# A transformer block in hyperbolic space on one core: one VectorE operation in place of two for q and k, and for the pair of gated MLP tiles

## The chip, the cores and the metric

The kernel runs on one core of a Trainium2 chip. The metric is the device time of one execution in microseconds (us), lower is better.

## The reference

The input x is 128 sequences of 64 tokens with 256 features, cond one row of 256 per sequence. All of it is float32. Vectors live in a ball: `logmap0` scales a vector by arctanh(norm)/norm, `expmap0` by tanh(norm)/norm, and a projection is `plin(x, w, b) = expmap0(logmap0(x) @ w + b)`. Cut to what matters:

```python
sh_msa, sc_msa, g_msa, sh_mlp, sc_mlp, g_mlp = split(t_emb @ w_ada + b_ada, 6)
xm = expmap0(layer_norm(logmap0(x)) * (1 + sc_msa) + sh_msa)
q, k, v = (_to_heads(plin(xm, w, b)) for w, b in ((w_q, b_q), (w_k, b_k), (w_v, b_v)))
qt, kt, vt = (logmap0(q), logmap0(k), logmap0(v))        # 16 heads of 16
attn = softmax(einsum('bhqd,bhkd->bhqk', qt, kt) / sqrt(16))
attn_out = plin(_from_heads(expmap0(attn @ vt)), w_o, b_o)
x1 = mobius_add(x, expmap0(g_msa * logmap0(attn_out)))
xm = expmap0(layer_norm(logmap0(x1)) * (1 + sc_mlp) + sh_mlp)
ff = plin(plin(xm, w_f1, b_f1), w_f2, b_f2)
out = x + mobius_add(x1, expmap0(g_mlp * logmap0(ff)))
```

In tangent space q, k and v of a head are the rows of the projection, each multiplied by one factor per token and head. That product for q and k is the first place of the change. The product `g_mlp * logmap0(ff)` is, up to a factor that is applied later, the second.

## The kernel before

A tile is 128 tokens (two sequences) by 256 features; there are 64. x stays in SBUF (`x_all`). The program has a setup (weights, the two MLP matrices folded into one, statistics of x), a loop over the 64 tiles for attention, a block of small operations on statistics of all tiles, and a loop over 32 pairs of tiles for the MLP and the output. Nothing is scheduled by a planner: each engine has its own stream of instructions, written by hand, and semaphores tie them together.

*Attention loop.* Slots are software-pipelined. In the slot of DVE (VectorE) in which tile n is modulated, tile n-4 gets its factors, n-6 is normalised and gated, and so on (`L_A` to `L_G`). DVE's order in a slot, each a function with one operation unless said otherwise: `limit` (L1202), `modulate` (L1081, needs rows of `mod` by DMA), `factors` (L1208), `scale_qk` (L1219, two operations), `shift_t` (L1127), `sum_squares` and `sum_rows` (L1149, L1153), `softmax_sums` (L1158), `clip_t` (L1134), `normalise` (L1163, writes `o`), `repeat_parts` (L1228, L1229), `project` (L1143, writes `u` from the qkv PSUM), `dot_x` (L1195), `gate_z` (L1188, needs the output projection in PSUM). PE (TensorE) in a slot: transpose of `t` (L839), the projection to q and k (L885), attention times v (L899), the projection to v (L885), then waits for `o` and transposes it (L850), the scores (L875) and the output projection (L856, L858), between which ScalarE copies the transposed `o` (L617). After `scale_qk`, ScalarE rounds q and k to 16 bit (L612) and GpSimd takes the rest (L478), both once for q and k together, after a wait for both. SP's queue issues, in this order in a slot, the rows of `mod` (L372), the transposing DMA of q and k (L379) and the rows of `gate` (L385). `modulate` and the sums go by tile parity in double buffers. DVE's stream is written out in full (its slots are unrolled in Python), PE's, ScalarE's, GpSimd's and SP's are hardware loops of two slots.

*MLP loop.* All engines are unrolled. DVE's order for a pair: `clip_t2` (L1354), `inner_square` for both tiles (L1362, needs PE's inner product), `inner_norm` (L1370), `first_sum` (L1273), `scale_t2` (L1282) and `shift_t2` (L1348) for both tiles of a later pair, `inner_factors` (L1376), `mlp_output` for both (L1384, writes `ff`), `gate_mlp` for both (L1393, reads `ff`), `dot_x1` for both (L1400, reads what was gated). Every fourth slot brings a chain of some twenty small operations on the factors of eight tiles (`output_norms`, `output_factors`, L1415 to L1446; called the fin chain here). ScalarE's order: scale x (L688), scale t2 by the clip (L714), diagonals (L744), copy of the transposed tile (L719), copy of the output (L749), squares of t2 (L707), of `ff` (L725) and of the gated tiles (L731). PE transposes (L933), multiplies (L947) and adds up the output (L959 to L961). 

The waits at the first place and at the second are these:

```python
dve.wait_ge(fac_ready, i + 1)          # scale_qk, before two operations
dve.wait_ge(ff_ready, n + 1)           # gate_mlp, n = 2 * i + j
dve.wait_ge(fg_ready, n + 1)           # dot_x1
```

Of the kernel before, what the change touches and what calls it, by code (L numbers as in the profile page):

```python
# [26 lines left out]
ALU = mybir.AluOpType  # L27
# [3 lines left out]
P = 128  # L31
# [21 lines left out]
def build(nc, x, cond, w_q, b_q, w_k, b_k, w_v, b_v, w_o, b_o, w_f1, b_f1, w_f2, b_f2, w_ada, b_ada, out):  # L53
    B, S, D = x.shape
    FF = w_f1.shape[1]
    H = 16
    HD = D // H
# [12 lines left out]
    with ExitStack() as ctx:  # L70
        def sb(name, shape, dt=F32):
            return ctx.enter_context(nc.sbuf_tensor(name, shape, dt))
# [4 lines left out]
        def sem(name):  # L77
            return ctx.enter_context(nc.semaphore(name))
# [12 lines left out]
        def scratch(n):  # L91
# [39 lines left out]
        u = sb("u", [P, 2, 3 * D])  # L131
# [10 lines left out]
        fac = sb("fac", [P, 3 * H])  # L142
        qk = sb("qk", [P, 2 * D])
# [19 lines left out]
        ff = qk[:, :].rearrange("p (j d) -> p j d", j=2)  # L163
        fgs = ([u[:, :, :].rearrange("p a n -> p (a n)")[:, 2 * D * n:2 * D * n + 2 * D] for n in range(3)]
               + [usq[:, 0:2 * D], tT[:, :, :, :].rearrange("p a c n -> p (a c n)"),
                  wqkv[:, :, :].rearrange("p c n -> p (c n)")[:, 4 * D:6 * D],
                  v[:, :, :, :].rearrange("p a h n -> p (a h n)")[:, 0:2 * D], wo[:, :, :].rearrange("p c n -> p (c n)")])
        fgs = [b.rearrange("p (j d) -> p j d", j=2) for b in fgs]
# [4 lines left out]
        gates2 = (gate[:, :, :], bqkv[:, 0:2 * D].rearrange("p (j d) -> p j d", j=2))  # L173
# [63 lines left out]
        qk_ready = sem("qk_ready"); high_ready = sem("high_ready"); low_ready = sem("low_ready"); again_ready = sem("again_ready"); v_ready = sem("v_ready")  # L237
# [17 lines left out]
        ff_ready = sem("ff_ready"); fg_ready = sem("fg_ready")  # L255
# [74 lines left out]
        def on2(h, off, lag):  # L330
            return not isinstance(h, int) or 0 <= TURN * h + off - lag < HALF
# [653 lines left out]
        def _(dve):  # L985
# [10 lines left out]
            n = T // 8  # L996
# [88 lines left out]
            part = lambda k: bn[:, :, k]  # L1085
# [126 lines left out]
            def scale_qk(i, k):  # L1212


                dve.wait_ge(fac_ready, i + 1)
                after(dve, low_ready, i)
                for a in range(2):
                    part = slice(a * D, a * D + D)
                    dve.tensor_tensor(qk[:, part].rearrange("p (h d) -> p h d", d=HD), u[:, k, part].rearrange("p (h d) -> p h d", d=HD),  # L1219
                                      fac[:, a * H:a * H + H].unsqueeze(2).broadcast_to([P, H, HD]), ALU.mult).then_inc(qk_ready, 1)  # L1220

            def repeat_parts(i, k, half):

# [160 lines left out]
                dve.scalar_tensor_tensor(out=ff[:, j, :], in0=(p_qkv, p_s)[k][:, 512 * j + P:512 * j + P + D], scalar=ch[:, j:j + 1],  # L1384
                                         in1=b2[:, :], op0=ALU.mult, op1=ALU.add).then_inc(ff_ready, 1)

            def gate_mlp(i, j, k, r, half):

                n = 2 * i + j
                dve.wait_ge(ff_ready, n + 1)  # L1390
                dve.wait_ge(gate2_in[k], 32 * half + 32)
                after(dve, out_psum, i - (TURN - 1))
                dve.tensor_tensor(fgs[r][:, j, :], ff[:, j, :], gates2[k][:, j, :], ALU.mult).then_inc(fg_ready, 1)  # L1393

            def dot_x1(i, j, r, q, col):

# [64 lines left out]
            def slot2(h, off):  # L1461
                slots = TURN * h + off
                if on2(h, off, M_Q):
                    clip_t2(slots - M_Q, (off - M_Q) % 2)
                if on2(h, off, M_B):
                    i, k = slots - M_B, (off - M_B) % 2
                    for j in range(2):
                        inner_square(i, j, k)
                    inner_norm(i)
                if on2(h, off, M_A):  # L1470
                    i, k = slots - M_A, (off - M_A) % 2
                    half = (TURN // 2) * h + (off - M_A) // 2
                    for j in range(2):
                        if not at_start(h, off):
                            first_sum(i, j)
                    for j in range(2):
                        if not at_start(h, off):
                            scale_t2(i, j, k, half)
                    for j in range(2):
                        shift_t2(i, j, k)  # L1480
                if group_at(h, off, M_P) is not None:
                    output_root(group_at(h, off, M_P))
                if on2(h, off, M_B):
                    i, k, r = slots - M_B, (off - M_B) % 2, (off - M_B) % TURN
                    half = (TURN // 2) * h + (off - M_B) // 2
                    q, col = parity(off, M_B), 2 * ((off - M_B) % GROUP)
                    inner_factors(i)
                    for j in range(2):
                        mlp_output(i, j, k)
                    for j in range(2):  # L1490
                        gate_mlp(i, j, k, r, half)
                    for j in range(2):
                        dot_x1(i, j, r, q, col)
                if group_at(h, off, M_N) is not None:
                    output_norms(group_at(h, off, M_N), parity(off, M_N))
                if group_at(h, off, M_P) is not None:
                    output_factors(group_at(h, off, M_P), parity(off, M_P))
# [25 lines left out]
```

## Time and profile before

| | |
|---|---|
| median of 3 runs | 765.44 us (763.75 to 766.3) |
| the profiled execution | 765.7 us |
| its span | 763.9 us |
| granted TensorE clock, mean | 0.945 |
| busy: PE, DVE, ACT, POOL | 84%, 86%, 69%, 45% of the span |
| attention loop | from about 55 to 490 us |
| MLP loop | from about 530 to 760 us |

In the profile PE is TensorE, DVE VectorE, ACT ScalarE, POOL GpSimd, SPq the DMA queue of SyncE. L1219 is line 1219 of the kernel. The shares are means over stages with different limits. "issue" is idle time in which an engine waited for nothing that the profile shows. A wait is put down to what came last. The profile's timeline joins neighbouring operations of one group in one row (x2), whose time is then that of all of them from first start to last end. The semaphore waits that stand as instructions of their own are not shown in it.

### The profile page before, as it was taken

What the parts mean: (1) busy time and instruction counts of PE and PEld (TensorE: products, weight loads), DVE (VectorE), ACT (ScalarE), POOL (GpSimd) and SP (SyncE); (2) the same over time, 40 slices, a digit from 0 to 9 for tenths busy, and PEclk for the clock granted to TensorE, in tenths of its full rate; (3) what the DMA queues carried; (4) which work ended last, traced back from release to release, by engine and by line L of the source; (5) the groups of instructions that cost most, each with busy time, mean ns of one, the idle gap of its engine ahead of it and who ended that gap; (6) DMA issues with size and microseconds to landing.
All of it is one profiled execution on the core that took longest, in us unless ns stands there. A gap on an engine that the chain in (4) does not pass through costs nothing. (4 is left out here: it accounts for less than half of the span.)

```text
span 763.9 us, 27111 instructions
## 1 busy us (share of the span) xinstructions
PE 644.4 (84%) x8419; PEld 464.3 (61%) x8433; DVE 654.1 (86%) x2171; ACT 524.7 (69%) x1563; POOL 347.0 (45%) x683
## 2 busy tenths in 40 slices
PE   4956889999999999999999997605669999999996
PEld 2645667777777777777777775402326566656664
DVE  2786788999999999999999997485998999999975
ACT  1123567777777777777777775334879989999874
POOL 1003556666666666666666665111234244234321
PEclk9978899999999999999999998656999999999999
DMA  9942876666666666666666665222444455445523
GB/s 321 359 116 57 141 131 137 146 141 143 141 147 142 145 142 147 141 141 144 147 140 147 144 133 113 50 70 70 124 124 133 139 158 163 149 132 166 164 72 110
DMA packets 184804, 107.50 MB, mean 141 GB/s; under 512 B 140188, under 2 KB 167591, under 8 KB 184744
## 3 DMA queue, kind: packets, MB, share of 16 engines
q1 hardware_dynamic: 182952, 103.99, 55.6%
q10 hardware_dynamic: 1792, 2.89, 1.0%
q8 instruction: 17, 0.28, 0.1%
q14 instruction: 43, 0.35, 0.1%
HBM read 64.11 MB, written 9.18 MB: 96 GB/s over the span
## 5 line engine op out<-in xcount | busy, mean ns | idle before, releaser
L885 PE MATMUL p_qkv<-wqkv,tT 128*128 128x256 f32 x768 | 198.1, 396 | 5.5 <-DVE u L1143 5.5
L885 PEld LDWEIGHTS p_qkv<-wqkv,tT 128*128 128x128 f32 x768 | 139.7, 195 | 22.9 <-issue 6.3
L899 PEld LDWEIGHTS p_o<-v,pT 64*64 64x64 f32 x4096 | 66.7, 136 | 21.9 <-issue 21.9
L899 PE MATMUL p_o<-v,pT 64*64 64x17 f32 x4096 | 73.0, 210 | 0.0
L858 PE MATMUL p_oz<-wo,oT 128*128 128x256 f32 x256 | 69.7, 397 | 0.0
L445 POOL TENSOR_TENSOR rt<-ss_t,c_mhalf 128x1 f32<-128x1 f32 x64 | 42.1, 658 | 60.6 <-ACT junk L634 53.7
L659 ACT ACTIVATE pT<-p_s 128x1024 f32<-128x1024 f32 x64 | 65.6, 1024 | 2.8 <-PE p_s L875 1.7
L1143 DVE SCALAR_TENSOR_TENSOR u<-p_qkv,ct,bqkv 128x768 f32<-128x768 f32 x64 | 64.3, 1005 | 3.5 <-PE p_qkv L885 3.5
L617 ACT ACTIVATE oT<-p_oz 128x256 f32<-128x256 f32 x64 | 24.6, 384 | 57.0 <-PE p_oz L850 57.0
L504 POOL TENSOR_TENSOR rt<-ss,c_mhalf 128x2 f32<-128x2 f32 x32 | 26.5, 827 | 80.8 <-ACT wqkv L707 80.8
L933 PE MATMUL p_t<-ident,pT 128*128 128x128 f32 x128 | 21.3, 290 | 46.5 <-ACT pT L714 46.5
L1149 DVE TENSOR_REDUCE hs<-usq 128x48 f32<-128x768 f32 x64 | 60.5, 945 | 0.0
L478 POOL TENSOR_TENSOR qk<-qk 128x512 f16<-128x512 f32 x32 | 37.0, 1156 | 51.4 <-ACT qk L612 51.4
L478 POOL TENSOR_TENSOR mod_b<-qk,mod_b 128x512 f16<-128x512 f32 x32 | 37.0, 1156 | 49.7 <-ACT mod_b L612 49.7
L510 POOL TENSOR_TENSOR rh<-hh,c_mhalf 128x2 f32<-128x2 f32 x32 | 27.3, 854 | 70.1 <-DVE hh L1370 70.1
L628 ACT ACTIVATE usq<-u 128x768 f32<-128x768 f32 x64 | 53.3, 833 | 6.2 <-DVE u L1143 6.2
L947 PE MATMUL p_qkv<-wff,qk 128*128 128x384 f32 (+1 forms) x128 | 53.4, 561 | 0.8 <-ACT qk L719 0.8
L947 PE MATMUL p_s<-wff,qk 128*128 128x384 f32 (+1 forms) x128 | 52.6, 555 | 0.9 <-ACT qk L719 0.9
L850 PE MATMUL p_oz<-ident,o 128*128 128x128 f32 x128 | 27.3, 296 | 29.8 <-DVE o L1163 14.8
L1219 DVE TENSOR_TENSOR qk<-u,fac 128x256 f32<-128x256 f32 x128 | 48.6, 421 | 2.2
L933 PEld LDWEIGHTS p_t<-ident,pT 128*128 128x128 f32 x128 | 13.8, 143 | 59.4 <-ACT pT L714 30.8
L858 PEld LDWEIGHTS p_oz<-wo,oT 128*128 128x128 f32 x256 | 46.4, 202 | 3.8
(275 smaller groups left out, 1685.2 us busy)
## 6 DMA issues: line engine op xcount, KB each, us to landing
mod<-mod_rows SPq DMA_DIRECT2D x128, 128.0 KB, 2.9
x_all<-in_x SPq DMA_DIRECT2D x8, 1024.0 KB, 14.3
gate<-mod_rows SPq DMA_DIRECT2D x128, 64.0 KB, 2.7
mod<-mod_rows SPq DMA_DIRECT2D x32, 256.0 KB, 4.2
mod_b<-mod_rows SPq DMA_DIRECT2D x32, 256.0 KB, 4.4
out<-x_all SPq DMA_DIRECT2D x32, 256.0 KB, 3.0
gate<-gate_rows SPq DMA_DIRECT2D x32, 128.0 KB, 2.9
bqkv<-gate_rows SPq DMA_DIRECT2D x32, 128.0 KB, 2.9
```

Source lines behind the costliest of these rows:

```text
L445: pool.tensor_tensor(rt[:, k:k + 1], ss_t[:, k:k + 1], c_mhalf[:, 0:1], ALU.pow).then_inc(rt_ready, 1)
L478: pool.tensor_tensor(low, qk[:, :].rearrange("p (a h d) -> p a h d", a=2, d=HD), big[:, :, :, 0, :], ALU.subtract).then_inc(low_ready, 1)
L628: act.activation(usq[:, :], u[:, k, :], ACT.Square).then_inc(u_squared, 1)
L659: act.activation(pT[:, :, :, :].rearrange("p e g n -> p (e g n)"), p_s[:, :], ACT.Exp, scale=SCALE / (QK_UP * QK_UP)).then_inc(p_ready, 1)
L858: mm = pe.matmul(p_oz[:, D:2 * D], oT[:, c, :, :].rearrange("p b s -> p (b s)"), wo[:, c, :], start=False, stop=c == C - 1)
L885: mm = pe.matmul(p_qkv[:, a * D:a * D + D], tT[:, k, c, :], wqkv[:, c, a * D:a * D + D], start=c == 0, stop=c == C - 1)
L899: mm = pe.matmul(p_o[S * e:S * e + S, col:col + VW], pT[keys, e, g, :], v[keys, k, 2 * g + e, :], start=True, stop=True, skip_group_check= ...
L933: mm = pe.transpose(p_t[:, m * P:m * P + P], t2s[:, k, m // 2, (m % 2) * P:(m % 2) * P + P], ident[:, :])
L947: mm = pe.matmul((p_qkv, p_s)[k][:, 512 * j + c * P:512 * j + 512], t2T[:, k, j, c, :], wff[:, c, c * P:2 * D], start=False, stop=c == C - 1)
L1143: dve.scalar_tensor_tensor(out=u[:, k, :], in0=p_qkv[:, 0:3 * D], scalar=ct[:, k:k + 1], in1=bqkv[:, :], op0=ALU.mult, op1=ALU.add).then_i ...
L1149: dve.tensor_reduce(hs[:, 0:3 * H], usq[:, :].rearrange("p (a d) -> p a d", d=HD), AX.X, ALU.add).then_inc(heads_summed, 1)
L1219: dve.tensor_tensor(qk[:, part].rearrange("p (h d) -> p h d", d=HD), u[:, k, part].rearrange("p (h d) -> p h d", d=HD), fac[:, a * H:a * H ...
```

## The change

`scale_qk` multiplies q and k (512 columns side by side in `u` and `qk`) by their factors in one operation and raises `qk_ready` by 2 at its end, instead of once after each half. `gate_mlp` gates both tiles of a pair in one operation, after a wait for both outputs, and raises `fg_ready` by 2. Nothing else is edited.

```diff
                 dve.wait_ge(fac_ready, i + 1)
                 after(dve, low_ready, i)
-                for a in range(2):
-                    part = slice(a * D, a * D + D)
-                    dve.tensor_tensor(qk[:, part].rearrange("p (h d) -> p h d", d=HD), u[:, k, part].rearrange("p (h d) -> p h d", d=HD),
-                                      fac[:, a * H:a * H + H].unsqueeze(2).broadcast_to([P, H, HD]), ALU.mult).then_inc(qk_ready, 1)
+                dve.tensor_tensor(qk[:, :].rearrange("p (h d) -> p h d", d=HD), u[:, k, 0:2 * D].rearrange("p (h d) -> p h d", d=HD),
+                                  fac[:, 0:2 * H].unsqueeze(2).broadcast_to([P, 2 * H, HD]), ALU.mult).then_inc(qk_ready, 2)
...
-            def gate_mlp(i, j, k, r, half):
-
-                n = 2 * i + j
-                dve.wait_ge(ff_ready, n + 1)
+            def gate_mlp(i, k, r, half):
+
+                dve.wait_ge(ff_ready, 2 * i + 2)
                 dve.wait_ge(gate2_in[k], 32 * half + 32)
                 after(dve, out_psum, i - (TURN - 1))
-                dve.tensor_tensor(fgs[r][:, j, :], ff[:, j, :], gates2[k][:, j, :], ALU.mult).then_inc(fg_ready, 1)
+                dve.tensor_tensor(fgs[r], ff[:, :, :], gates2[k], ALU.mult).then_inc(fg_ready, 2)
...
-                    for j in range(2):
-                        gate_mlp(i, j, k, r, half)
+                    gate_mlp(i, k, r, half)
```

On DVE in the attention loop the stream was, with the semaphores that each operation waits for in brackets (those beyond the first are instructions of their own):

```order
L1202 TENSOR_TENSOR rlim<-roots,c_lim 128x3 [waits fac_ready,roots_ready]
L1081 SCALAR_TENSOR_TENSOR lnx<-x_all,arrays,mod 128x256 [waits t_ready,mod_in1]
L1208 TENSOR_TENSOR fac<-roots,rlim 128x48 [waits v_ready,qk_ready,rlim_ready]
L1219 TENSOR_TENSOR qk<-u,fac 128x256 [waits low_ready,fac_ready]
L1219 TENSOR_TENSOR qk<-u,fac 128x256
L1127 SCALAR_TENSOR_TENSOR t<-lnx,arrays,mod 128x256 [waits t_squared,tT_psum,ln_half]
L1149 TENSOR_REDUCE hs<-usq 128x48 [waits roots_ready,u_squared]
```

and is now, in the same place:

```order
L1202 TENSOR_TENSOR rlim<-roots,c_lim 128x3 [waits fac_ready,roots_ready]
L1081 SCALAR_TENSOR_TENSOR lnx<-x_all,arrays,mod 128x256 [waits t_ready,mod_in1]
L1208 TENSOR_TENSOR fac<-roots,rlim 128x48 [waits v_ready,qk_ready,rlim_ready]
L1217 TENSOR_TENSOR qk<-u,fac 128x512 [waits low_ready,fac_ready]
L1127 SCALAR_TENSOR_TENSOR t<-lnx,arrays,mod 128x256 [waits t_squared,tT_psum,ln_half]
L1149 TENSOR_REDUCE hs<-usq 128x48 [waits roots_ready,u_squared]
```

One instruction is gone, its neighbours stand as before. In the MLP loop DVE's stream for a pair was

```order
L1376 TENSOR_SCALAR ch<-rh 128x2 [waits ff_ready,rh_ready]
L1384 SCALAR_TENSOR_TENSOR qk<-p_qkv,ch,b 128x256 [waits fg_ready,ff_squared,ch_ready] x2
L1393 TENSOR_TENSOR u<-qk,gate 128x256 [waits gate2_in0,ff_ready] x2
L1400 SCALAR_TENSOR_TENSOR junk,fst<-g_all,u 128x256 [waits xf_summed,fg_ready] x2
L1354 TENSOR_SCALAR ct<-rt 128x2 [waits t2s_ready,rt2_ready]
```

and is now

```order
L1374 TENSOR_SCALAR ch<-rh 128x2 [waits ff_ready,rh_ready]
L1382 SCALAR_TENSOR_TENSOR qk<-p_qkv,ch,b 128x256 [waits fg_ready,ff_squared,ch_ready] x2
L1390 TENSOR_TENSOR u<-qk,gate 128x512 [waits gate2_in0,ff_ready]
L1397 SCALAR_TENSOR_TENSOR junk,fst<-g_all,u 128x256 [waits xf_summed,fg_ready] x2
L1352 TENSOR_SCALAR ct<-rt 128x2 [waits t2s_ready,rt2_ready]
```

The line numbers behind each edit fall by two, then by three. The streams of the other engines are unchanged.

## Rows read from the trace of the kernel before

**Rows 1.** The page, busy us (share of the span) xinstructions
```profile
PE 644.4 (84%) x8419; PEld 464.3 (61%) x8433; DVE 654.1 (86%) x2171; ACT 524.7 (69%) x1563; POOL 347.0 (45%) x683
```

**Rows 2.** By stage: length, busy PE, PEld, DVE, ACT, POOL, PEclk, DMA share, GB/s
```profile
119.61:451.74 332.13, 311.67 (x6086) 240.55 (x6085) 313.05 (x938) 248.95 (x677) 213.04 (x469) 1.00 0.65 144
601.04:628.80 27.76, 26.45 (x104) 17.21 (x105) 25.97 (x103) 25.56 (x90) 10.34 (x10) 1.00 0.52 152
534.38:557.77 23.39, 16.05 (x53) 7.34 (x53) 22.81 (x85) 19.21 (x69) 7.58 (x9) 1.00 0.48 130
```

**Rows 3.** Timeline of DVE: start, us, line, operation, tiles, count
```profile
304.85 0.20 DVE L1208 TENSOR_TENSOR fac<-roots,rlim 128x48 f32<-128x48 f32 x1
...
311.43 0.20 DVE L1208 TENSOR_TENSOR fac<-roots,rlim 128x48 f32<-128x48 f32 x1
...
314.00 0.09 DVE L1134 TENSOR_SCALAR ct<-rt 128x1 f32<-128x1 f32 x1
314.12 0.42 DVE L1163 TENSOR_TENSOR o<-p_o,rden 128x256 f32<-128x256 f32 x1
...
316.86 0.42 DVE L1188 SCALAR_TENSOR_TENSOR g_all<-p_oz,gate 128x256 f32<-128x256 f32 x1
...
317.68 0.20 DVE L1208 TENSOR_TENSOR fac<-roots,rlim 128x48 f32<-128x48 f32 x1
317.92 0.76 DVE L1219 TENSOR_TENSOR qk<-u,fac 128x256 f32<-128x256 f32 x2
318.60 0.47 DVE L1127 SCALAR_TENSOR_TENSOR t<-lnx,arrays,mod 128x256 f32<-128x256 f32 x1
```

**Rows 4.** Timeline of PE; in brackets idle time before, and what ended it
```profile
308.54 0.41 PE L850 MATMUL p_oz<-ident,o 128*128 128x128 f32 x2 [0.61 <-DVE o L1163]
...
314.79 0.41 PE L850 MATMUL p_oz<-ident,o 128*128 128x128 f32 x2 [0.16 <-issue]
```

**Rows 5.** Waits in 119.6 to 457.7 us: in total, times, longest
```profile
DVE rden L1158 <- issue: 3.0, 13, 0.2
DVE lnx L1081 <- DMA mod<-mod_rows: 1.4, 4, 0.5
```

**Rows 6.** DMA queues in 119.61 to 451.74 us: packets, MB, share
```profile
q14 instruction: 13, 0.11, 0.1%
```

**Rows 7.** Timeline of ACT in the MLP loop
```profile
625.54 0.91 ACT L714 ACTIVATE pT<-qkT,ct 128x256 f32<-128x256 f32 x2 [1.07 <-DVE ct L1354]
...
630.59 0.40 ACT L731 ACTIVATE wqkv<-v 128x256 bf16<-128x256 f32 x1
```

**Rows 8.** Timeline of DVE in the MLP loop
```profile
629.00 0.88 DVE L1384 SCALAR_TENSOR_TENSOR qk<-p_qkv,ch,b 128x256 f32<-128x256 f32 x2
629.79 0.75 DVE L1393 TENSOR_TENSOR v<-qk,gate 128x256 f32<-128x256 f32 x2
630.46 0.42 DVE L1400 SCALAR_TENSOR_TENSOR junk<-g_all,v 128x256 bf16<-128x256 f32 x1
...
631.93 0.42 DVE L1362 SCALAR_TENSOR_TENSOR wqkv<-p_s,pT 128x256 bf16<-128x256 f32 x1 [0.28 <-PE p_s L947]
```

**Rows 9.** Groups by line and shape: xcount, busy us, mean ns, idle before
```profile
L1143 DVE SCALAR_TENSOR_TENSOR u<-p_qkv,ct,bqkv 128x768 f32<-128x768 f32 x64 | 64.3, 1005 | 3.5 <-PE p_qkv L885 3.5
...
L1219 DVE TENSOR_TENSOR qk<-u,fac 128x256 f32<-128x256 f32 x128 | 48.6, 421 | 2.2
...
L1384 DVE SCALAR_TENSOR_TENSOR qk<-p_qkv,ch,b 128x256 f32<-128x256 f32 x32 | 14.0, 480 | 0.6
```

**Rows 10.** Timeline of DVE at two stalls
```profile
307.14 0.20 DVE L1153 TENSOR_REDUCE hs<-hs 128x3 f32<-128x48 f32 x1
307.57 0.26 DVE L1158 RECIPROCAL rden<-p_o 128x16 f32<-128x16 f32 x1 [0.23 <-issue]
...
460.38 0.09 DVE L1134 TENSOR_SCALAR ct<-rt 128x1 f32<-128x1 f32 x1
460.74 0.42 DVE L1163 TENSOR_TENSOR o<-p_o,rden 128x256 f32<-128x256 f32 x1 [0.27 <-DVE rden L1158]
```

## The prediction

> **What bounds the kernel now.** I first read where the time lies. The summary says that VectorE (DVE) is the busiest engine with 86% of the span, TensorE (PE) close behind with 84% [rows 1]. That is a mean over three stages, so the table by stage comes next [rows 2]. The attention loop has 64 tiles, and 52 of its slots take 332.13 us, 6.39 us each. The MLP loop repeats itself every four slots, in 27.76 us, once it has settled. In each stretch PE and DVE are both about 94 to 97% busy, so busy shares can't say who is waiting for whom. The waits and the order in time must.
>
> Attention loop. I followed one slot on DVE [rows 3] and on PE [rows 4]. DVE writes o (L1163) until 314.54; PE starts the transpose L850 at 314.79; after the scores, a copy on ScalarE and the projection L858 DVE's gate_z (L1188) starts at 316.86. From the end of o to gate_z is 2.32 us, in which DVE has other work but none that the change touches. From gate_z to the next end of o DVE is never idle for more than some 0.04 us, and scale_qk (L1219) stands there. From one L1208 to the next (311.43, 317.68) is 6.25 us. So the slot is one ring: PE and ScalarE from o to gate_z (2.32 us), DVE from gate_z to o (the other 3.93 us). PE idles 0.16 us before L850 [rows 4]: if DVE gets faster, PE is the next limit at some 0.16 us less a slot.
>
> Two things lengthen some slots [rows 5]. In 13 of the 52 slots DVE sits before L1158 for 0.23 us although nothing that the profile shows is missing ("issue"), then PE waits for o and DVE for z; such a slot takes 6.58 us (304.85 to 311.43 in [rows 3]), 0.33 more. It is every fourth slot, at the same instruction. In the same stretch there are 13 instruction fetches of 0.11 MB in all [rows 6], one for each of them. And in some slots L1081 waits for the rows of mod, up to 0.5 us [rows 5]. The sum closes: 52 x 6.25 + 13 x 0.33 = 329.3, and 2.8 us are left for late mod transfers and odd slots.
>
> MLP loop. DVE's fin chain (factors of 8 tiles) comes once in four slots. After it ScalarE waits 1.07 us for DVE's clip (L1354) [rows 7]; for about two slots ahead of that DVE is never idle, so its work is the path. In the other two slots ScalarE and PE set the pace and DVE waits for PE before the second L1362 (0.28 us in [rows 8]). In the first slots DVE is the bound: 22.81 of 23.39 us in four of them [rows 2].
>
> **The change, part by part.**
>
> *Scaling q and k.* Removed: 64 times, two operations of 256 columns, 421 ns each [rows 9]; added: one of 512. From the first L1219 to L1127 is 0.67 to 0.68 us [rows 3], since an operation that waits for nothing starts some 0.08 us before the one ahead of it ends. The row for 512 columns is missing. The projections of 768 and 256 columns give the slope, (1005 - 480) / 512 = 1.03 ns a column [rows 9]. So the new one takes 421 + 256 x 1.03 = 684 ns, less the overlap of 0.08: 0.60 to 0.61 us. Gain 0.065 us a slot (bounds: 0 if columns cost more than this, 0.1). It lies in the DVE part of the ring and is under PE's 0.16. q comes no later for its readers, since both ScalarE (L612) and GpSimd (L478) wait for q and k together anyway. 52 x 0.065 = 3.4 us. On the Trainium skill, page "VectorE: DVE Perf Modes", section on the TRN2 errata: a tensor_tensor of 512 fp32 elements measured 691 ns; with that the gain is 0.058 a slot, 3.0 us.
>
> Of this something goes back: a shorter slot gives the mod transfers less time. SP issues them behind the transpose and the gate rows, and they arrive close to their use already [rows 5]. I take back 0.035 us in each second slot, 0.9 us; bounds 0 and all of it for these slots, 1.7 us.
>
> *The stall every fourth slot.* It sits at a fixed distance in instructions, and the change takes one out of each slot's 32 (16 operations, the rest separate waits and accumulator reads). So it will no longer meet L1158 each time, but move four instructions on with each fourth slot. What it costs then depends on what DVE executes meanwhile. Behind L1153 and L1134, operations of 0.2 and 0.09 us, it shows: 0.43 and 0.36 us from start to start [rows 10], where L1134 to L1163 is 0.12 else [rows 3]. Behind one of 0.6 to 1.0 us (L1143, L1149, the new L1217) some 0.4 us is covered, and between o and gate_z the ring has about 0.1 us of slack. Going round by fours I count 5 or 6 of 14 places with 0.2 to 0.4 us and the others near 0: some 1.7 us where 14 x 0.33 = 4.6 are paid now. Gain 2.9 us less what falls on slots with a late mod; I take 2.1. Bounds: 0 (each costs what it does now) and 4.6. The Trainium skill ("Runtime: NRT & Kernel Launch", section on instruction fetch mechanics) calls a block crossing mostly hidden and gives blocks of 16 KiB; the rows show 8 KB each and a price, so the rows decide.
>
> Attention loop in sum: 3.4 - 0.9 + 2.1 = 4.6 us gained, bounds 1.3 and 8.
>
> *Gating a pair.* Removed: two operations of 0.42 us per slot, 0.67 us from the first's start to L1400 [rows 8]; added: one of 0.68. But now neighbours depend on each other. Today's order is output 0, output 1, gate 0, gate 1, dot 0, dot 1: each waits for the last but one, and they overlap. The new gate waits for output 1 directly ahead of it, and dot 0 for the gate directly ahead of it. What a direct wait costs is in [rows 3]: L1208 ends at 317.88 and L1219, which needs it, starts at 317.92, 0.04 us after the end instead of 0.08 before. Worked out on [rows 8]: output 1 ends at 629.88, the gate runs from 629.92 to 630.60, dot 0 starts at 630.64 instead of 630.46. That is 0.18 us later in every slot, though one operation less. The queue behind it is dot 0, dot 1, the fin chain and the clip for which ScalarE waits; ScalarE's square of the gated tile (L731) starts today at 630.59 [rows 7] and would get its data at 630.60 + 0.04: 0.05 us late where ScalarE sets the pace.
>
> In which slots does it count? The first six, where DVE leads: 6 x 0.18 = 1.1. The two DVE slots of each of six groups: 12 x 0.18 = 2.2. The slots after the clip, by ScalarE: 5 x 0.05 = 0.25. The last two, which end in a serial chain: 0.2. In the others DVE waits for PE by 0.28 us or more, which covers it. Sum 3.7 us lost; bounds 2 (half the pairs covered) and 4.9 (all slots of the loop at 0.15). The Trainium skill ("VectorE: DVE Perf Modes", section on the DRAIN) says that a semaphore between chained Vector operations costs nothing extra and that only their number counts. By it this part gains; that is rival 3.
>
> *Sum.* -4.6 + 3.7 = -0.9 us. The profiled execution took 765.7 us, the median of the other three 765.44; from the median that is **764.5 us**. A measurement of this kernel tells 0.3% (2.3 us) from nothing, so this counts as no change.
>
> **Rivals.**
> 1. *The stalls stay as dear as they are.* Gain in the attention loop only 2.5 us, net +1.2: 766.6. For it: the fetch is the same, and the stall has been seen in only two places. Against: in [rows 10] it is shorter in the second of them.
> 2. *The mod transfers become the bound (slower).* If the rows of every second tile land just when L1081 wants them, half of the slots keep their time: gain 1.7 us, and the moved stalls only change places with waits for mod. With 4.6 us lost in the MLP loop the net is +2.9: 768.3. It decides once the spare time of these transfers is under 0.065 us; four waits of up to 0.5 us in 52 slots [rows 5] say that some are there already, and the 6.25 us slots that most are not.
> 3. *Only the number of operations counts (faster).* Then a direct wait costs nothing, and the 18 slots where DVE is the path each give 0.07 us: -4.6 - 1.2 = -5.8, 759.6 us. Against it: the 0.04 us after the end of L1208 in [rows 3], which is the same in every slot that I read.
> 4. *Nothing gained in the attention loop, PE being the limit:* +3.7, 769.1. Against: the 0.61 us that PE idles when o is late, and L850 always 0.25 us behind o [rows 3, 4].
>
> **Numbers.** Forecast 0.52 (its own range 762 to 767.5), rival 1 0.20, rival 2 0.12, rival 3 0.11, rival 4 0.05. The range of 761.3 to 768.3 leaves out rival 3, rival 4 and the edge of rival 2. Faster by over 0.3% (below 763.1): rival 3 and a quarter of the forecast, 0.25. Slower (above 767.7): rivals 2 and 4 and a little of 1 and of the forecast, 0.20. Within 0.3%: 0.55.
>
> **What would show it.** Right: L1217 at 680 to 690 ns and a plain attention slot of 6.19 us; the "issue" stalls spread over other lines, fewer waits of PE for o, more of L1081 for mod; in the MLP loop the gate 0.04 us behind output 1's end, dot 0 as far behind the gate, four slots in 28.1 to 28.2 us instead of 27.76. Wrong: plain slots still at 6.25 (PE or another cycle bounds), 13 stalls at one line again, or four MLP slots in 27.76 us or less.

## The result, and the profile after

The changed kernel takes **769.66 us** (median of 5 runs, 768.67 to 772.0); the kernel before, on the same chip, 765.05 (5 runs, 763.75 to 766.3). The ratio is 1.0074 with a 95% interval of 1.005 to 1.0097: 4.6 us slower, and outside the predicted range. The profiled execution took 769.66 us as well, its span is 767.9.

By stage, on the same pieces of the program as in [rows 2], the length stands first, then the busy time of PE, PEld, DVE, ACT and POOL, the granted clock, DMA share and GB/s:

```profile
116.09:447.79 331.70, 311.67 (x6086) 240.60 (x6085) 311.69 (x886) 248.79 (x677) 213.22 (x469) 1.00 0.65 144
571.79:600.22 28.43, 25.60 (x102) 16.79 (x103) 26.41 (x99) 25.33 (x89) 10.28 (x10) 1.00 0.47 140
628.86:658.75 29.89, 28.12 (x109) 18.30 (x110) 26.39 (x99) 25.85 (x90) 10.08 (x10) 0.98 0.47 141
658.75:687.22 28.47, 26.64 (x104) 17.35 (x105) 26.37 (x99) 25.80 (x90) 10.60 (x10) 1.00 0.51 149
```

The 52 attention slots take 331.7 us where they took 332.1 [rows 2]: 0.4 gained, not 4.6. DVE executes 52 operations fewer (886, not 938), as it should. (The slots are counted from L1208 of the 8th tile to L1208 of the 60th.) Four MLP slots take 28.3 to 28.6 us and once 29.89, where one group of [rows 2] takes 27.76. Over the whole MLP loop, from the first ch (L1376, now L1374) to the 32nd, it is 219.8 us against 210.2: 9.6 longer. Of this the first six slots have 4.6 (43.0 against 38.4), the twenty after them 4.3 and the last five 0.6. The MLP loop starts 5.6 us earlier than before: the attention loop starts at the same time, but its first seven slots and the filling ahead of them took 3.5 us less in this execution, and the operations between the loops 1.3 us. Most of that belongs to the execution and not to the change, for the kernel before, profiled once more (e0), starts its MLP loop 5.9 us earlier too.

DVE around the merged scaling of q and k. The columns are those of [rows 3]:

```profile
223.97 0.20 DVE L1208 TENSOR_TENSOR fac<-roots,rlim 128x48 f32<-128x48 f32 x1
224.26 0.69 DVE L1217 TENSOR_TENSOR qk<-u,fac 128x512 f32<-128x512 f32 x1
```

The merged operation takes 0.69 us, as forecast (684 ns). But it starts 0.09 us after the end of L1208, where L1219 followed 0.04 us behind it in [rows 3]. The median over the tiles is 0.091 us, and was 0.034. So the slot keeps its length: from L1208 to L1208 a plain slot is 6.24 us, not 6.19.

DVE at the merged gate of the first MLP slot, and ScalarE's square behind it:

```profile
528.96 0.88 DVE L1382 SCALAR_TENSOR_TENSOR qk<-p_qkv,ch,b 128x256 f32<-128x256 f32 x2
529.93 0.69 DVE L1390 TENSOR_TENSOR u<-qk,gate 128x512 f32<-128x512 f32 x1
530.66 0.42 DVE L1397 SCALAR_TENSOR_TENSOR junk<-g_all,u 128x256 bf16<-128x256 f32 x1
```
```profile
530.66 0.42 ACT L731 ACTIVATE wqkv<-u 128x256 bf16<-128x256 f32 x1 [0.27 <-DVE u L1390]
```

From the start of output 0 (L1382) to dot 0 (L1397) it is 1.70 us; in [rows 8] it was 1.46 (629.00 to 630.46). That is 0.24 more where the prediction had 0.18. Here too the gap in front of the merged operation is 0.09 us (528.96 + 0.88 = 529.84 to 529.93), that behind it 0.04.

The waits of DVE in the attention loop (in total, times, longest; 119.6 to 445 us), against [rows 5]:

```profile
DVE lnx L1081 <- DMA mod<-mod_rows: 3.7, 11, 1.1
DVE qk L1217 <- issue: 0.4, 1, 0.4
DVE g_all L1188 <- PE p_oz L858: 0.4, 1, 0.4
DVE ct L1134 <- issue: 0.2, 1, 0.2
DVE u L1143 <- issue: 0.2, 1, 0.2
```

The 13 "issue" waits at L1158 are gone, though the stage still has 13 instruction fetches (columns as in [rows 6]):

```profile
q14 instruction: 13, 0.11, 0.1%
```

Three such waits remain visible, at three different lines. In their place L1081 waits for the rows of mod 11 times (it was 4 times), 3.7 us in all and up to 1.1. The view leaves out idle times under 0.15 us. In the records of the trace, L1081 starts 0.074 us after the start of L1202 in a plain slot; by this measure it is late in 22 of the 52 slots, by 5.9 us in all, and before it was late in 11, by 2.6 us.

Three stretches of the MLP loop ran at the lower clock, and there the DVE waits for PE (same columns as the stages above; then DVE):

```profile
534.00:538.00 4.00, 3.74 (x7) 1.80 (x6) 3.38 (x13) 3.65 (x15) 0.69 (x1) 0.57 0.33 89
548.00:552.00 4.00, 3.75 (x7) 1.84 (x7) 3.39 (x12) 3.65 (x16) 0.69 (x1) 0.57 0.34 90
561.50:565.50 4.00, 3.75 (x7) 1.70 (x6) 3.81 (x13) 2.84 (x12) 1.26 (x2) 0.57 0.27 70
```
```profile
537.95 0.42 DVE L1360 SCALAR_TENSOR_TENSOR wqkv<-p_qkv,pT 128x256 bf16<-128x256 f32 x1 [0.46 <-PE p_qkv L947]
539.51 0.42 DVE L1360 SCALAR_TENSOR_TENSOR wqkv<-p_qkv,pT 128x256 bf16<-128x256 f32 x1 [1.13 <-PE p_qkv L947]
```

The second and the fourth slot of the loop take 7.75 and 7.72 us, 5.97 each in the profile of before. That looks like a part of the loss. It had to be tested whether it belongs to the change at all.

### The profile page after: what moved, and what is told of

It is laid out like the page before. It is cut to its first block and busy times, and to the rows that moved or that the text cites. A ratio compares the mean times of both kernels' runs of the same rounds, so it can differ in the third digit from the quotient of the medians.

```text
span 767.9 us, 27008 instructions
## 1 busy us (share of the span) xinstructions
PE 646.1 (84%) x8419; PEld 465.3 (61%) x8433; DVE 656.1 (85%) x2075; ACT 525.7 (68%) x1563; POOL 346.3 (45%) x683
## 5 line engine op out<-in xcount | busy, mean ns | idle before, releaser
L947 PE MATMUL p_qkv<-wff,qk 128*128 128x384 f32 (+1 forms) x128 | 57.6, 598 | 0.8 <-ACT qk L719 0.8
L1217 DVE TENSOR_TENSOR qk<-u,fac 128x512 f32<-128x512 f32 x64 | 44.3, 693 | 6.2 <-issue 0.4
```

What stands on the lines that cost most here:

```text
L947: mm = pe.matmul((p_qkv, p_s)[k][:, 512 * j + c * P:512 * j + 512], t2T[:, k, j, c, :], wff[:, c, c * P:2 * D], start=False, stop=c == C - 1)
L1217: dve.tensor_tensor(qk[:, :].rearrange("p (h d) -> p h d", d=HD), u[:, k, 0:2 * D].rearrange("p (h d) -> p h d", d=HD), fac[:, 0:2 * H].un ...
```

## The experiments

**What was open.** My theory after the result: the two merged operations start late because their semaphore is raised by 2. The records of the trace, one line for each instruction, show a difference that the diff does not. This is the changed kernel, in the order of DVE's stream (start, end in us on the profile's time, line; `>=` waits, `+=` and `++` raise; 157 is fac_ready, 158 qk_ready, 160 low_ready):

```
223.966 224.166 TENSOR_TENSOR 1208 $S[153]>= $S[157]++
223.701 224.212 EVENT_SEMAPHORE    $S[160]>= $S[157]>=
224.257 224.950 TENSOR_TENSOR 1217 $S[158]+=
```

The operation that raises by 2 has no wait of its own. The one for fac stands ahead of it, in the separate wait instruction that was there for low_ready before. That instruction ends 0.046 us after L1208, and L1217 starts 0.045 us later. Rival: 512 columns, or one operation instead of two, cause it, whatever the raise.

The timed results, in us. "Attention" is the 52 slots, "gap" from the end of L1208 to qk, "out to dot" from output 0 to dot 0, from each run's trace. "Late mod" adds up by how much L1081 starts late in the 52 slots, by the measure above, with the number of slots. The kernel before was run again in each session (medians 763.8 for the first four, 764.76 for e0, e6, e7 and e11, 763.15 for the last four).

| kernel | median (range, runs) | ratio to before (95%) | attention | late mod | gap | MLP loop | out to dot |
|---|---|---|---|---|---|---|---|
| before, profile | | 1 | 332.1 | 2.6 (11) | 0.034 | 210.2 | 1.46 |
| the change | 769.66 (768.67-772.0, 5) | 1.0074 (1.005-1.0097) | 331.7 | 5.9 (22) | 0.091 | 219.8 | 1.69 |
| e1_qk_only | 764.85 (762.84-767.84, 12) | 1.0025 (1.0009-1.0041) | 330.7 | 4.8 (18) | 0.091 | 212.8 | 1.46 |
| e2_gate_only | 768.53 (766.3-771.5, 6) | 1.0063 (1.0045-1.0082) | 332.3 | 2.5 (14) | 0.034 | 218.2 | 1.69 |
| e3_qk_by_one | 760.14 (758.66-761.03, 6) | 0.9955 (0.9938-0.9972) | 330.0 | 7.4 (25) | 0.034 | 213.4 | 1.46 |
| e4_both_by_one | 763.87 (761.37-765.4, 12) | 1.0003 (0.999-1.0015) | 328.1 | 5.5 (21) | 0.034 | 215.8 | 1.64 |
| e0_before_again | 761.95 (1) | | 332.1 | 2.5 (13) | 0.034 | 212.3 | 1.46 |
| e6_fac_by_two | 764.06 (762.81-765.35, 12) | 0.9994 (0.9978-1.001) | 333.2 | 6.7 (19) | 0.035 | 210.1 | 1.46 |
| e7_qk1_sp | 750.31 (748.66-751.75, 6) | 0.9816 (0.979-0.9842) | 322.2 | 0.0 (1) | 0.035 | 213.4 | 1.46 |
| e11_sp | 758.3 (756.13-759.2, 6) | 0.9914 (0.9887-0.994) | 329.5 | 0 | 0.034 | 213.5 | 1.46 |
| e14_change_sp | 761.65 (758.29-762.83, 12) | 0.9971 (0.9949-0.9994) | 325.9 | 0.2 (2) | 0.091 | 219.7 | 1.69 |
| e13_waits_sp | 765.34 (763.2-768.28, 12) | 1.0023 (1.0004-1.0042) | 335.8 | 0.2 (1) | 0.202 | 212.5 | 1.46 |
| e10_qk1_sp_dots | 748.02 (746.9-749.65, 6) | 0.9795 (0.977-0.982) | 322.2 | 0.0 (1) | 0.034 | 210.3 | (moved) |
| e9_dots_gate1 | 751.58 (750.43-751.99, 6) | 0.9838 (0.9814-0.9862) | 322.3 | 0.0 (1) | 0.034 | 213.7 | (moved) |

**e1_qk_only**: the change without its gate part.

```diff
-                for a in range(2):
-                    part = slice(a * D, a * D + D)
-                    dve.tensor_tensor(qk[:, part]..., ALU.mult).then_inc(qk_ready, 1)
+                dve.tensor_tensor(qk[:, :]..., ALU.mult).then_inc(qk_ready, 2)
```

> Only the merge of q and k, as in the change (qk_ready raised by 2). Theory A (the loss sits in the MLP loop; in the attention loop the merge itself gives 0.01 us a slot, because its wait became an instruction of its own, and the fetch stalls that move off L1158 give some 3 us): 2 to 4 us faster than before, 761 to 763, plain attention slots at 6.24 to 6.25 us, MLP loop as before (27.76 us per four slots). Theory B (the change costs in both loops, the attention gain seen in the profile was noise of the setup): 765 to 767.

Measured 764.85, ratio 1.0025: no gain from the part that should have brought 4.6, rather a small loss. Theory A had the plain slot right and the time wrong (761 to 763). The wait for the rows of mod is 2.9 us in 10 times, the stalls at L1158 are gone, a plain slot is 6.24. Its profiled execution, 762.84 us, was the lowest of the twelve, so that its trace shows this part better than it is.

**e2_gate_only**: the other half.

```diff
-                    for j in range(2):
-                        gate_mlp(i, j, k, r, half)
+                    gate_mlp(i, k, r, half)
...
+                dve.tensor_tensor(fgs[r], ff[:, :, :], gates2[k], ALU.mult).then_inc(fg_ready, 2)
```

> Only the merge of the two gates, as in the change (fg_ready raised by 2). Theory A (two direct waits of 0.12 us each and one wait on its own in every slot: 0.24 us where VectorE leads, plus slots in which the TensorE clock falls to its lower level): 6 to 9 us slower than before, 771 to 774; dot 0 starts 1.70 us after output 0 instead of 1.46. Theory B (most of the loss in the MLP loop was the fall of the clock, which comes and goes by chance): 3 to 5 us slower in the median, with runs that spread by 3 us or more.

Measured 768.53, ratio 1.0063, 4.7 us lost; the attention loop keeps its time (332.3), and in the MLP loop four slots take 28.37 us. Dot 0 comes 1.69 us after output 0, as theory A had it, but the time is theory B's: a part of the MLP loss in the profiles was the clock (e0 below). The two halves multiply to 1.0088, inside the interval of the change. The gate carries most of the loss.

**e3_qk_by_one**: as e1, but the semaphore is raised by 1 and those who wait for it count by one.

```diff
-                  ....then_inc(qk_ready, 2)
+                  ....then_inc(qk_ready, 1)
...
-                pool.wait_ge(qk_ready, 2 * i + 2)
+                pool.wait_ge(qk_ready, i + 1)
...
-                after(dve, qk_ready, 2 * i - 2)
+                after(dve, qk_ready, i - 1)
```

> Merge of q and k, qk_ready raised by 1 and its thresholds halved. Theory A (a raise by 2 drives the wait for fac off the operation into an instruction of its own, which costs 0.055 us on the ring): L1217 starts 0.04 us after L1208 ends instead of 0.09, plain slots at 6.19 us; of this half or more goes to waits for the rows of mod, so 1 to 2 us faster than e1. Rival (the longer operation itself starts later, whatever its semaphore does): gap stays at 0.09 us, time as e1.

This decides where the operation starts. The record of e3 at the same place:

```
305.958 306.650 TENSOR_TENSOR 1217 $S[157]>= $S[158]++
```

The operation now carries its wait for fac itself, and on DVE's timeline it follows as closely as L1219 did:

```profile
305.72 0.20 DVE L1208 TENSOR_TENSOR fac<-roots,rlim 128x48 f32<-128x48 f32 x1
305.96 0.69 DVE L1217 TENSOR_TENSOR qk<-u,fac 128x512 f32<-128x512 f32 x1
306.57 0.48 DVE L1127 SCALAR_TENSOR_TENSOR t<-lnx,arrays,mod 128x256 f32<-128x256 f32 x1
```

Plain slots take 6.19 us, as the prediction had it, and the kernel 760.14: 4.7 us less than e1 in the same session, for the same arithmetic in the same order, and more than the 1 to 2 us expected. The rival falls: the shape is the same in both. The Trainium skill ("Trainium Kernel Development and Optimization", section on key constraints) says that compute semaphores increment by 1; it gives no reason and I had not weighed it. The runs show that raising by 2 works and what it costs here. What the two profiles show is less than 4.7: their spans differ by 2.2 us (761.0 and 758.8), and their 52 slots by 0.7. The slots should give 52 x 0.055 = 2.9, but 2.6 of it went to the rows of mod, late by 7.4 us instead of 4.8. The profile of e1 was that kernel's lowest execution, so most of the rest lies in the spread between executions; it was not placed. With the transfers out of the way (e14 by 2, e7 by 1, both below) the same step is worth 3.7 us in the 52 slots (325.9 against 322.2; the gates of the MLP loop play no part there), 52 x 0.055 = 2.9 of it by the gap.

**e4_both_by_one**: both merges, both semaphores by 1.

```diff
-                dve.tensor_tensor(fgs[r], ...).then_inc(fg_ready, 2)
+                dve.tensor_tensor(fgs[r], ...).then_inc(fg_ready, 1)
...
-                    act.wait_ge(fg_ready, n + 1)
+                    act.wait_ge(fg_ready, i + 1)
```

> Both merges, both semaphores raised by 1. Theory A: the attention loop as e3, in the MLP loop 0.18 instead of 0.24 us a slot; 2.5 to 4 us faster than the change, 766 to 767. Rival (raising by 2 costs nothing): as the change, 769.5.

Measured 763.87, ratio 1.0003: the whole change, with only the raise mended, costs nothing. By the ratios that is some 5.4 us under the change, where 2.5 to 4 were expected. Here the first gate:

```profile
524.67 0.88 DVE L1382 SCALAR_TENSOR_TENSOR qk<-p_qkv,ch,b 128x256 f32<-128x256 f32 x2
525.58 0.69 DVE L1390 TENSOR_TENSOR u<-qk,gate 128x512 f32<-128x512 f32 x1
526.30 0.43 DVE L1397 SCALAR_TENSOR_TENSOR junk<-g_all,u 128x256 bf16<-128x256 f32 x1
```

The gate starts 0.03 us behind output 1 (524.67 + 0.88 = 525.55 to 525.58), not 0.09, and dot 0 comes 1.63 us after output 0: 0.17 more than before, close to the 0.18 of the prediction. Four MLP slots take 28.17 us, inside the 28.1 to 28.2 of the prediction. From e3 to e4, the gate merge alone, it is 3.7 us; by 2 (e2) it is 4.7. That 1 us between them is within the noise of the times; what shows it is the slots, 28.17 and 28.37 us for four.

**e0_before_again**: the kernel before, unchanged, with a profile of its own.

> The kernel before, profiled once more. In its first profile the TensorE clock fell once in the MLP loop (571 to 575 us); in the four kernels with a merge that were profiled it fell three times, near 534, 548 and 562 us, also where the MLP loop's program is that of before. Theory A (the falls come from where the loop starts against the last low stretch, whatever was edited, and vary between executions): falls in the first 40 us of the MLP loop here too, at other places than in the first profile, its MLP loop 1 to 4 us longer than the 210.2 us of the first. Theory B (the kernel before does not have them): one fall, 210.2 us again.

The table by stage, around the first two clock falls of its MLP loop:

```profile
532.50:536.50 4.00, 3.92 (x10) 1.83 (x11) 3.96 (x13) 3.07 (x14) 1.10 (x2) 0.58 0.62 158
546.20:550.20 4.00, 3.75 (x8) 1.66 (x6) 3.50 (x13) 3.77 (x15) 0.70 (x1) 0.57 0.38 117
```

The falls to 1.2 GHz in the first MLP slots are there without the change, and the second and fourth slot take 7.25 and 7.58 us. The first profile of before had but one fall in this loop, at 571 us. So of the 9.6 us by which the loop looked longer, 2.1 belong to the executions compared (212.3 against 210.2). What is left is 7.5, slot against slot: 1.7 in one slot with a clock fall more, at 626.7 us, in the group of 29.89 us above, and 5.8 in the others, mostly 0.20 to 0.25 us in a slot that DVE leads (up to 0.5 in a few) and near 0 to 0.17 in the rest. e14 has that fall as well, 98 us after its MLP loop starts, as in the change; e2, whose MLP loop is the same program, has not. With it ScalarE's L749 waits 1.4 us for PE, and the slot takes 7.79 us instead of 6.1. It is one profile of each kernel, so how often the fall comes is not known.

**e6_fac_by_two**: the kernel before, with only the semaphore of L1208 raised by 2 (and its waits doubled).

```diff
-                ..., ALU.min).then_inc(fac_ready, 1)
+                ..., ALU.min).then_inc(fac_ready, 2)
-                dve.wait_ge(fac_ready, i + 1)
+                dve.wait_ge(fac_ready, 2 * i + 2)
```

> The kernel before with no merge at all; only fac_ready, raised by factors (L1208) and waited for behind it, is raised by 2 and its thresholds doubled. Theory A (an operation that raises by 2 can't carry its own wait for rlim_ready, which becomes an instruction of its own): the gap ahead of L1208 (behind L1081) does not matter, since rlim is ready long before, so 0 to 1 us; but a slot has one instruction more or less and the fetch stalls may leave L1158: up to 3 us faster. Rival (each raise by 2 costs 0.05 us wherever it stands): 3.3 us slower, 767.

Measured 0.9994, a plain slot stays at 6.25, and L1208 still starts 0.083 us before L1081 ends. So a raise by 2 costs nothing where the waits ahead of the operation are long met: L1208 waits for rlim, which L1202 writes two operations earlier. It costs where the wait that it displaces is for the operation directly ahead. The extra instruction (33 in a slot instead of 32) also moved the stalls off L1158, but L1081 was late for mod by up to 0.8 us, 6.7 in all, and that took the gain: 333.2 us.

**e7_qk1_sp**: e3, and SP issues the gate rows of a tile behind the next rows of mod instead of ahead of them.

```diff
-                if on(h, off, L_H):
-                    i, k = 2 * h + off - L_H, (off - L_H) % 2
...
+                if on(h, off, L_H + 1):
+                    i, k = 2 * h + off - (L_H + 1), (off - (L_H + 1)) % 2
                     after(sp, zg_ready, i - 1)
                     for b in range(TB):
                         sp.dma_start(gate[...], mod_row(i, b, 2 * D, 3 * D)).then_inc(gate_in[k], 16)
```

> As e3 (q and k merged, raised by 1), and SP issues the rows of gate one slot later, behind the rows of mod, so that mod no longer queues behind gate. Theory A (in e3 every second slot waits for mod, 0.3 us in the mean): these waits vanish, slots at 6.19 us but for few stalls; attention slots 7 to 59 in 323 to 325 us instead of 330.0, 5 to 6 us faster than e3, 754 to 755. Rival (another cycle binds at the same place, the transfers' time shifts to gate and gate_z waits): 759 to 760.

Measured 750.31, 4 us better than expected. The waits of DVE in the loop (119.6 to 445 us):

```profile
DVE g_all L1188 <- PE p_oz L858: 6.9, 25, 0.5
DVE rden L1158 <- PE p_o L899: 0.5, 1, 0.5
DVE u L1143 <- issue: 0.3, 2, 0.2
DVE mod_b L1226 <- issue: 0.2, 1, 0.2
DVE ct L1134 <- issue: 0.2, 1, 0.2
```

No wait for mod is left, nearly all slots take 6.18 or 6.19 us and the 52 take 322.2. The same merge without the SP order (e3) takes 330.0, 7.8 more, of which the late starts of L1081 are 7.4. Some 2.6 us of such waits were there before; the other 5.2 are what these transfers kept of the gain of the merge and the moved stalls.

**e11_sp**: the kernel before with the SP order of e7 alone.

> The kernel before with only the order on SP changed (rows of gate behind rows of mod). Theory A: the 2.8 us that late mod transfers take in slots 7 to 59 go away, the 13 stalls at L1158 stay: 2 to 3 us faster than before, 761. Rival: no difference, 763.8.

```profile
DVE g_all L1188 <- PE p_oz L858: 4.2, 13, 0.3
DVE rden L1158 <- issue: 3.0, 13, 0.2
```

Measured 758.3, ratio 0.9914, 6.5 us faster where 2 to 3 were expected. In the 52 slots it is 2.6 us, which is what the sum of the prediction had left for late rows of mod (2.8). The first seven slots, outside of them, take 43.6 us instead of 45.5 (e0) or 49.0 (the first profile of before), which is most of the rest as far as it was placed. All 13 stalls stay at L1158. From e11 to e7, the merge by 1 alone with the transfers out of the way, it is 7.3 us in the 52 slots: 52 x 0.065 = 3.4, and some 3.9 of the 4.3 that the stalls cost.

**e14_change_sp**: the change with the SP order.

> The change itself (both merges, raised by 2) with SP's rows of gate behind those of mod. Theory A (the fetch stalls that left L1158 gave back some 3.7 us, and waits for mod took it all): attention slots 7 to 59 in 325 to 326 us instead of 331.7, all of 6.24 us but a few; 5 to 7 us faster than the change, 763. Rival (the stalls' gain was small): 328 us or more, 766.

Measured 761.65, ratio 0.9971, and 325.9 us in the attention loop against 331.7, as theory A had it. So 5.8 us of the changed kernel's loop are waits for mod, which agrees with the 5.9 us of late starts. By the ratios the kernel is some 8 us faster than the change, more than the 5 to 7 expected; in the two profiles the first seven slots give 2.9 us besides. Without the waits for mod the 52 slots are 52 x 6.24 = 324.5 and 1.4 more for the stalls that still show.

**e13_waits_sp**: e11, with two more waits ahead of L1219, on semaphores that reached their value long before the loop (L1219 is L1221 there). It should shift the stalls without merging anything; a slot has 33 instructions.

```diff
+                dve.wait_ge(ones_set, 1)
+                dve.wait_ge(ident_made, 2)
                 dve.wait_ge(fac_ready, i + 1)
```

> No merge: the kernel before with SP's new order and two more waits, on semaphores that are long reached, ahead of scale_qk. They add one instruction to each slot, 33 instead of 32. Theory A (the stall belongs to every 128th instruction and stays at L1158 only because 4 slots are 128 instructions): the stalls leave L1158, most are covered, slots 7 to 59 in 326 to 327 us instead of 329.5 (e11), 755 to 756. Rival (the stall belongs to what happens at L1158 every fourth slot, not to the count; the merges removed it otherwise): 13 stalls at L1158 again, 758 or more.

```profile
301.42 0.20 DVE L1208 TENSOR_TENSOR fac<-roots,rlim 128x48 f32<-128x48 f32 x1
301.82 0.76 DVE L1221 TENSOR_TENSOR qk<-u,fac 128x256 f32<-128x256 f32 x2 [0.20 <-DVE fac L1208]
302.50 0.47 DVE L1127 SCALAR_TENSOR_TENSOR t<-lnx,arrays,mod 128x256 f32<-128x256 f32 x1
```

The time missed what I expected: 765.34. The stalls did leave L1158 (one "issue" wait of 0.2 us there instead of 13), so their place does hang on the number of instructions in a slot. But the two waits widened the gap behind L1208 from 0.034 to 0.20 us, and a plain slot takes 6.42. The records (columns as above; 115 and 130 are among the semaphores that were met long ago) show how:

```
301.421 301.622 TENSOR_TENSOR 1208 $S[153]>= $S[157]++
301.661 301.682 EVENT_SEMAPHORE    $S[157]>=
301.730 301.780 EVENT_SEMAPHORE    $S[160]>= $S[115]>=
301.824 302.249 TENSOR_TENSOR 1221 $S[130]>= $S[158]++
```

That is the mechanism of the raise by 2, larger: the wait for fac has lost its place on the operation, and a second wait instruction stands behind it. A met wait as such is free, also ahead of a dependent operation: in the kernel before, the one for low_ready stands ahead of L1219 and is over before L1208 starts (317.418 to 317.439 us). The cost comes when the wait for the operation directly ahead leaves the operation that needs it.

**e10_qk1_sp_dots**: e7, and both dots of an MLP pair stand behind the next slot's clip (L1352), for which ScalarE waits; gates not merged.

```diff
-                    for j in range(2):
-                        dot_x1(i, j, r, q, col)
...
                 if on2(h, off, M_Q):
                     clip_t2(slots - M_Q, (off - M_Q) % 2)
+                if on2(h, off, M_B + 1):
+                    i, r = slots - (M_B + 1), (off - (M_B + 1)) % TURN
+                    for j in range(2):
+                        dot_x1(i, j, r, parity(off, M_B + 1), 2 * ((off - (M_B + 1)) % GROUP))
```

> As e7, and in the MLP loop both dots of a pair stand behind the next pair's clip, 0.69 us of VectorE's work that ScalarE need not wait for. No merge of gates. Theory A (in two of four slots VectorE's work up to the clip is the path): ScalarE's wait of 1.07 us falls to about 0.4, a group of four slots takes 27.1 to 27.4 us instead of 27.76, 746 to 748. Rival (the work must be done anyway ahead of the following waits): 27.7 us, 750.

ScalarE's waits for the clip, 600 to 700 us, of the changed kernel and then of e10:

```profile
ACT pT L714 <- DVE ct L1352: 4.6, 3, 1.6
```
```profile
ACT pT L714 <- DVE ct L1352: 1.6, 4, 0.5
```

These two differ in more than the dots; in e7, from which e10 is made, it is 4.3 us in 4 waits of up to 1.1. Measured 748.02 us, 2% under the kernel before and the fastest here. Four MLP slots take 27.48 us, 0.3 less than in e7, though theory A had 27.1 to 27.4. Against e7 the times alone don't tell: ratios of 0.9795 and 0.9816, with intervals that overlap.

**e9_dots_gate1**: e10 with the gates merged, raised by 1.

> As e10, and the gates merged with fg_ready raised by 1. No dot stands directly behind the gate now, the gate still does directly behind output 1. Theory A (each direct wait costs 0.12 us, the merged operation saves 0.065): 0.05 us a slot where VectorE leads, 0 to 1.5 us slower than e10. Rival (the longer operation costs by holding back ScalarE's square of tile 0): 2 us or more slower than e10.

Measured 751.58, 3.6 us slower than e10, with four slots in 27.88 us. With the dots out of the way, the merged gate has one direct wait left, on output 1, instead of two, and the merge still loses. That goes to the rival in my expectation, not to the theory, which had 1.5 us at most. The records bear the rival out. In the two slots of four that DVE leads, the merge costs 0.02 and 0.05 us, as the theory had it; in the two that ScalarE leads, 0.11 and 0.21. In the first of these ScalarE's square of tile 0 (L731) starts 1.33 us after output 0 in e10, where tile 0's gate is over at 1.21. In e9 it starts at 1.64, 0.04 behind the end of the gate of both tiles at 1.60. Those 0.31 us are what ScalarE, busy without a pause from there on, is late by in the next slot. So besides its direct waits the merged gate has a second price, the later first half. With the dots in their old place (e4) ScalarE comes to that square later anyway (1.59 us without the merge), and it costs 0.05.

## Why the prediction was wrong

By its own steps:

- **"Gain 0.065 us a slot" for q and k: it failed in the changed kernel, by the start of the operation and not by its length.** L1217 takes 693 ns (684 forecast). The 691 ns that the Trainium skill has ("VectorE: DVE Perf Modes", section on the TRN2 errata) were nearer. I took over the gap of 0.04 us behind L1208 from [rows 3]. Raised by 2, the gap is 0.09, and that is 0.055 of the 0.065. The diff showed the raise, and it was read as mere counting. By 1 (e3) the gap is 0.034 and the slot 6.19: the arithmetic of the step was right.
- **"I take back 0.9 us" for the mod transfers: mis-sized, 3.3 us.** L1081 was late by 2.6 us in the 52 slots before and by 5.9 in the changed kernel (by e11 and e14, 2.6 and 5.8). This is rival 2's mechanism. I had even bounded it at 1.7, by the slots' gain of 0.065 alone. But every 0.33 us that a stall had cost was spare time for the rows of mod as well, so what the moved stalls gave was taken too. Four waits of up to 0.5 us in [rows 5] were seen and priced as rare; the records have 11 late slots there.
- **Stalls, "Gain 2.9 us less what falls on slots with a late mod; I take 2.1": right in kind.** (The 4.6 us from which it starts count 14 stalls; [rows 5] has 13, 4.3 us.) They left L1158, most are hidden, and with the transfers out of the way the gain is about 2.9 to 3.9 (the 1.4 us left in e14, the 3.9 of e11 to e7). In the changed kernel it does not reach the time.
- **Attention loop in sum, 4.6 gained: 0.4 measured.** Part by part: 0.5 from the slots (forecast 3.4), 2.9 from the stalls (2.1), 3.3 lost to mod (0.9). It closes: before, 52 x 6.25, 13 x 0.33 and 2.6 of mod are 331.9; after, 52 x 6.24, 1.4 for the stalls (from e14) and 5.9 of mod are 331.8.
- **The gate, "0.18 us later in every slot", 3.7 lost: right for a raise by 1** (0.17 to 0.18 a slot and 3.7 us, e3 to e4). As changed, the raise by 2 makes it 0.24 and 4.7 us (e2), on the edge of my bound of 4.9, which took 0.15 for every slot and so less than my own 0.18. Two direct waits do cost more than an operation saves. Rival 3, by which only the number of operations counts, falls: 32 fewer, and 3.7 us slower (e3 to e4). The Trainium skill ("VectorE: DVE Perf Modes") has no extra cost for a semaphore between chained copies in its section on the DRAIN, and its rules for kernel authors say to save operations, not semaphores. For this chain the traces do not agree: the merged gate starts 0.034 us after output 1 ends (e4), where the unmerged one started 0.084 before it.
- **The other rivals.** Rival 1, stalls as dear as ever, falls: they cost 1.4 us in e14 instead of 4.3. Rival 2 named what happened in the attention loop, waits for mod in the place of stalls; its 768.3 lies 1.4 under the result because it kept 1.7 us of gain where 0.4 was left. Rival 4, PE the limit, falls: at 6.19 us (e3, e7) PE keeps up. Its number, 769.1, was near the result by accident.
- **Not foreseen: the clock.** The falls in the first MLP slots are common to both kernels (e0). One more fall costs some 1.7 us in the profiles of the change and of e14. Whether it follows from the late clip (PE waited 1.96 us for ScalarE just before it) or from chance was not tested.

The result is thus the loss of the gate that I had, 3.7 and about 1 more, with next to nothing of the attention loop's gain to set against it.

## What to carry to other kernels

Before two operations become one, look at how the new one is counted and whom it follows: keep the raise at 1 and let the readers count anew, for a raise by 2, or waits that push the one for the operation directly ahead into an instruction of its own, put 0.06 to 0.17 us in front of it. Merge operations where neighbours in the queue are independent; between a producer and its reader two alternating operations hide the latency that one exposes, and that was worth more here than the operation saved. Ask also who reads the first half, for the merged operation gives it out only with the second (e9). And where a transfer already lands close to its use, first give it room (here one move in SP's queue, 0.9 to 1.4% of the time), since until then it swallows what the engines gain.

## What the runs showed of the hardware

- A VectorE operation that raises its semaphore by 2 does not carry its own wait (L1217 and L1390 of the change, L1208 in e6). The start behind a direct producer moves from 0.034 to 0.091 us after the producer's end, and the plain slot from 6.19 to 6.24 us (e3, e1); the two kernels differ by 4.7 us, of which the slots explain 3.5 at most.
- Two waits that were already met, added ahead of the wait for the producer, left two wait instructions between producer and reader and moved the start to 0.20 us (e13). Ahead of an operation whose data are long there, one such instruction more cost nothing (e6).
- An independent operation starts some 0.08 us before its predecessor's end [rows 3], a dependent one 0.03 to 0.04 us after: each direct wait costs 0.12 us.
- The stall of an instruction fetch is tied to a place in the stream: with 32 instructions in a slot it comes 13 times at the same line in 52 slots. One instruction fewer in each slot (31 in e1, e3, e7) or one more (33 in e6, e13) moves it, mostly to where it does not show.
- Two executions of the same kernel differed in where the clock fell, by 2.1 us in the MLP loop (before and e0). A stage's length needs more than one profile before a difference of this size is put down to a change.
